# A hybrid transformer kernel: steps may cross iterations, 26 down products formed from parts, low parts shared out anew

## Chip, cores and metric

One core of a Trainium2 chip runs the whole kernel in one launch. The metric is the device time of one execution in microseconds (us). The engines are TensorE (PE, with its weight loads listed as PEld), VectorE (DVE), ScalarE (ACT), GpSimd (POOL) and SyncE (SP, which only issues DMAs here).

## What is computed

The input is x of 8 sequences by 512 tokens by 128 channels, in float32. The reference, cut to its frame:

```
x = x + attention(layernorm(x))       # one causal head, d = 128
x = x + ffn(layernorm(x))             # layer 0
x = x + rwkv_block(layernorm(x))      # time mixing (wkv recurrence), then channel mixing, residual inside
x = x + ffn(layernorm(x))             # layer 1, the same weights as layer 0

ffn(x): softmax router over 32 experts, the top 4 with a capacity limit; each expert is
        (silu(x W1) * (x W3)) W2 * weight, with W1, W3 of 128x64 and W2 of 64x128;
        plus a shared expert of hidden width 128
```

## The kernel before

**Units and iterations.** Two experts are put side by side to make a hidden width of 128, so a feed-forward layer is 16 pairs plus the shared expert: 17 *units* (`UNITS`). One *iteration* `g` of 0 to 15 is the feed-forward layer of one sequence: g = 0 to 7 is layer 0 of the eight sequences, 8 to 15 is layer 1. All pairs are computed for all 512 tokens, with the routing weight multiplied in (it is zero where an expert was not chosen).

**One unit** goes through the engines so: TensorE forms the gate product in bank `pa` and the linear product in bank `pb` (`up`, L1039, L1040, L1043); ScalarE applies SiLU to `pa` (L732; or tanh, L734, after which VectorE completes it, L1449); VectorE multiplies by `pb` (`gate`, L1468 or L1471, giving `m_v`); GpSimd multiplies by the routing weights (`unit`, L587, giving `m_h`). The down product with W2 is then added up in the one bank `py` over the 17 units (`out_product`, L1045).

**Float32 by parts.** A product is either *plain* (a float32 matmul, which the trace lists as two matmul instructions, `py<-m_h,...` L1067) or *from parts*: each operand is a high part in `fp32r` plus a low remainder, and three `fp32r` matmuls are added, high by high, low weight by high, high weight by low (L1072, L1073, L1074). All up products are from parts. For a down product from parts the hidden tile has to be divided first: ScalarE copies `m_h` to the high part `m_hh` (`split_high`, L909, instruction at L921) and VectorE or GpSimd subtracts it to get the low part `m_hl` (`split_low`, L412, instruction at L416). A plain down product needs neither. `NATIVE[g]` lists the units with plain down products: 88 of the 272 before. `LOW_ON_POOL[g]` lists the units whose low part is GpSimd's, if they have one (64 of the 184 divided units; 120 are VectorE's). `LOW_LATE[g]` says which of VectorE's low parts stand after the unit's gate instead of before it, and `TANH[g]` which units use tanh (52).

**Rings.** `m_h` has 5 buffers, `m_hh` and `m_hl` have 3 each; the high part is made two units behind (`SPLIT_LAG`), the down product stands four units behind (`LAG`). Up products of unit p wait for the SiLU and the gate of unit p-2.

**Everything else is interleaved by hand.** Beside the units, an iteration carries other sequences' steps, as `plan(g)` says: attention of sequence g+2 (g < 6), the routing of iteration g+1 (`pro`), the begin, finish and out of time mixing (`begin`, `finish`, `out`), channel mixing (`cmix`). Each engine's program is written in *slots*: three to a unit (`PARTS`), 54 to an iteration (51 on TensorE). Every step has a tuple with one slot number for each of its occurrences, and is issued in that engine's queue when the loop comes to that slot. Before, the steps of `plan(g)` could only stand in iteration g. An engine runs its queue in order, so a step that waits for a semaphore holds what is behind it. Ahead of the iterations stands the *opening*, 40 slots of its own: the attention of sequences 0 and 1, the routing of sequence 0, the division of the weights into parts (`weights_step`) and the first two units' up products (`first_step`). `keep_clock` puts filler matmuls in the opening (22 in all by `FILL`); the fillers are not changed.

**DMA.** All loads and stores are issued on SP's queue in a fixed order that has no slots: input 0, w1, w3, input 1, the gate matrix, w2 and so on; then for every iteration the routing weights go out and come back broadcast over partitions.

**Functions that the change's steps touch:** `iteration` on each of four engines (L677, L936, L1346, L1805), `att_step` (L1482 on VectorE), `weights_step` (L1509 on VectorE, L611 on GpSimd), `pro_step`, `time_begin`, `time_finish`, `time_out`, `channel_step`, `first_step`.

## Time and profile before

| what | value |
|---|---|
| median of 3 runs | 792.92 us (792.66 to 793.96) |
| span of the profiled execution | 791.7 us (no other time is given for it) |
| PE busy | 785.1 us, 99% of the span |
| DVE, POOL, ACT busy | 645.9 (82%), 625.3 (79%), 567.9 us (72%) |
| mean granted TensorE clock | 1.000 of full speed |
| moved by DMA | 80.73 MB, mean 102 GB/s |

A busy share is the time in which an engine has an instruction under way, also where that instruction waits for a resource after it has begun. Matmuls are pipelined: the time given for one matmul holds the passage through the array, so the distance from the start of one to the start of the next, where neither waits, tells what it costs. Where an instruction follows a long one, its listed start can lie before the moment at which its columns enter, and the start after it has to be used.

### The profile page before, as it was taken

The numbers are of one execution on the slowest core, as the hardware profiler recorded it, in microseconds if no ns is written. First come the engines' busy times: TensorE is split into PE (matmuls) and PEld (weight loads), VectorE is DVE, ScalarE is ACT, GpSimd is POOL, SyncE is SP. The second block draws the span as 40 slices with busy tenths as digits, with TensorE's granted clock in tenths as the row PEclk, the third lists the DMA queues.
The fourth block names the chain that finished last, engine by engine and source line by source line (L and its number), as shares of the span: only waits on it lengthen the run. The fifth ranks groups of instructions, "written<-read, shape, count | busy, mean of one in ns | idle before, by whom it ended". The sixth has DMA issues, their size and how long they took to land.

```text
span 791.7 us, 12780 instructions
## 1 busy us (share of the span) xinstructions
PE 785.1 (99%) x3817; PEld 596.4 (75%) x3817; DVE 645.9 (82%) x1539; ACT 567.9 (72%) x1055; POOL 625.3 (79%) x491
## 2 busy tenths in 40 slices
PE   8999999999999999999999999999999999999998
PEld 5777778676776777768778777887778767788786
DVE  6875577997997989998988869988689889767686
ACT  5677787868768778689765867668685775677553
POOL 6687779849767797769987888998797877876985
PEclk9999999999999999999999999999999999999999
DMA  9353334243144342462425444253444424425552
GB/s 326 95 123 82 87 92 113 66 102 92 42 113 113 73 105 54 110 133 58 120 60 134 104 93 107 65 143 79 110 113 95 90 68 110 111 59 115 124 127 74
DMA packets 49332, 80.73 MB, mean 102 GB/s; under 512 B 3280, under 2 KB 14544, under 8 KB 48880
## 3 DMA queue, kind: packets, MB, share of 16 engines
q1 hardware_dynamic: 48976, 79.72, 42.1%
q8 instruction: 31, 0.51, 0.3%
q14 instruction: 37, 0.30, 0.1%
q10 hardware_dynamic: 288, 0.20, 0.1%
HBM read 75.19 MB, written 4.72 MB: 101 GB/s over the span
## 4 chain that ended last, share of the span: by engine, by line
PE 51%; POOL 2%; issue 2%; DVE 1%; ACT 0%; DVEq 0%; POOLq 0%; ACTq 0%
PE pa L1039 5%; PE pb L1039 4%; PE py L1067 4%; PE pa L1043 4%; PE pb L1043 4%; PE pa L1040 4%; PE pb L1040 4%; PE pu L1326 4%; PE py L1072 3%; PE py L1074 3%; PE py L1073 3%; POOL m_h L587 1%; PE pq L1283 1%; PE pu L1310 1%; PE pv L1334 1%
## 5 line engine op out<-in xcount | busy, mean ns | idle before, releaser
L587 POOL TENSOR_TENSOR m_h<-m_v,m_wb 128x512 f32<-128x512 f32 x254 | 364.3, 1444 | 98.7 <-DVE m_v L1468 42.9
L732 ACT ACTIVATE m_th<-pa 128x512 f32<-128x512 f32 x220 | 130.6, 594 | 102.0 <-PE pa L1043 97.7
L1468 DVE TENSOR_TENSOR m_v<-m_th,pb 128x512 f32<-128x512 f32 x205 | 138.6, 679 | 23.9 <-ACT m_th L732 15.5
L1039 PE MATMUL pa<-m_xh,w1h 128*128 128x512 f32 x272 | 137.2, 504 | 0.3 <-DVE m_v L1471 0.2
L416 DVE TENSOR_TENSOR m_hl<-m_h,m_hh 128x512 fp32r<-128x512 f32 x120 | 111.4, 929 | 24.8 <-ACT m_hh L921 24.1
L921 ACT ACTIVATE m_hh<-m_h 128x512 fp32r<-128x512 f32 x184 | 115.2, 626 | 13.8 <-POOL m_h L587 13.1
L1039 PE MATMUL pb<-m_xh,w3h 128*128 128x512 f32 x272 | 115.4, 424 | 0.0
L1043 PE MATMUL pa<-m_xl,w1h 128*128 128x512 f32 x272 | 107.3, 394 | 0.3 <-POOL m_xl L608 0.3
L1043 PE MATMUL pb<-m_xl,w3h 128*128 128x512 f32 x272 | 107.1, 394 | 0.0
L1040 PE MATMUL pa<-m_xh,w1l 128*128 128x512 f32 x272 | 106.6, 392 | 0.0
L1040 PE MATMUL pb<-m_xh,w3l 128*128 128x512 f32 x272 | 106.5, 391 | 0.0
L416 POOL TENSOR_TENSOR m_hl<-m_h,m_hh 128x512 fp32r<-128x512 f32 x64 | 86.1, 1345 | 12.6 <-ACT m_hh L921 12.1
L1072 PE MATMUL py<-m_hh,w2h 128*128 128x512 f32 x183 | 77.2, 422 | 0.0
L1074 PE MATMUL py<-m_hl,w2h 128*128 128x512 f32 x183 | 72.0, 394 | 0.0
L1073 PE MATMUL py<-m_hh,w2l 128*128 128x512 f32 x183 | 71.6, 392 | 0.0
L1039 PEld LDWEIGHTS pa<-m_xh,w1h 128*128 128x128 f32 x272 | 51.5, 189 | 25.5 <-issue 14.4
L1040 PEld LDWEIGHTS pa<-m_xh,w1l 128*128 128x128 f32 x272 | 51.5, 189 | 20.6 <-issue 14.6
L1039 PEld LDWEIGHTS pb<-m_xh,w3h 128*128 128x128 f32 x272 | 51.3, 189 | 14.0 <-issue 3.9
L1043 PEld LDWEIGHTS pa<-m_xl,w1h 128*128 128x128 f32 x272 | 51.1, 188 | 12.2 <-POOL m_xl L608 0.7
L1043 PEld LDWEIGHTS pb<-m_xl,w3h 128*128 128x128 f32 x272 | 51.1, 188 | 11.6
L1040 PEld LDWEIGHTS pb<-m_xh,w3l 128*128 128x128 f32 x272 | 51.4, 189 | 10.8 <-issue 1.9
L1449 DVE SCALAR_TENSOR_TENSOR m_th<-m_th,pa 128x512 f32<-128x512 f32 x52 | 35.2, 677 | 15.9 <-ACT m_th L734 15.8
(318 smaller groups left out, 1653.8 us busy)
## 6 DMA issues: line engine op xcount, KB each, us to landing
m_wb<-w_scratch SPq DMA_DIRECT2D x126, 512.0 KB, 6.5
x_sb<-in_x SPq DMA_DIRECT2D x8, 256.0 KB, 7.2
m_wb<-in_w SPq DMA_DIRECT2D x2, 1024.0 KB, 6.8
x_out<-x_sb SPq DMA_DIRECT2D x7, 256.0 KB, 6.6
u_scratch<-t_u SPq DMA_DIRECT2D x6, 256.0 KB, 2.6
t_u<-u_scratch SPq DMA_DIRECT2D x6, 256.0 KB, 2.7
f_kk<-in_w SPq DMA_DIRECT2D x1, 1024.0 KB, 9.7
w_scratch<-r_wT SPq DMA_DIRECT2D x16, 64.0 KB, 1.5
```

The lines of the kernel that those rows point to most:

```text
L416: eng.tensor_tensor(m_hl[:, at, :], hidden(g, p), m_hh[:, at, :].bitcast(F32), ALU.subtract)\
L587: pool.tensor_tensor(hidden(g, p), gated(g, p), m_wb[:, p % (GRING * GP), :], ALU.mult).then_inc(sig["m_h"], 1)
L732: ins = act.activation(m_th[:, p % 2, :], pa[p % 2][:, :], ACT.Silu)
L921: act.activation(m_hh[:, halves_at(g, p), :], hidden(g, p), ACT.Copy).then_inc(sig["m_hh"], 1)
L1039: pe.matmul(ps[:, :], high[:, p, :], xh, start=True, stop=False)
L1040: pe.matmul(ps[:, :], low[:, p, :], xh, start=False, stop=False)
L1043: return pe.matmul(ps[:, :], high[:, p, :], xl, start=False, stop=True)
L1072: pe.matmul(py[:, :], w2h[:, p, :], hh, start=(p == 0), stop=False)
L1073: pe.matmul(py[:, :], w2l[:, p, :], hh, start=False, stop=False)
L1074: pe.matmul(py[:, :], w2h[:, p, :], hl, start=False, stop=(p == last_down(g))).then_inc(sig["m_y"], 1)
L1449: dve.scalar_tensor_tensor(out=m_th[:, r, :], in0=m_th[:, r, :], scalar=1.0, in1=pa[r][:, :], op0=ALU.add, op1=ALU.mult).then_inc(sig["m_u ...
L1468: dve.tensor_tensor(gated(g, p), m_th[:, r, :], pb[r][:, :], ALU.mult).then_inc(sig["m_v"], 1)
```

## The change

New is `STAGE`, the 54 slots of an iteration. Each engine's `iteration` no longer runs the steps of its own plan alone but also those of the plans before and after, with the slot moved by 54: a slot below 0 stands in the iteration ahead, one of 54 or more in the iteration behind.

```diff
+STAGE = PARTS * (UNITS + 1)
...
+def beside(g):
+
+    return tuple((plan(g + d), -d * STAGE) for d in (-1, 0, 1) if 0 <= g + d < 2 * B)
...
-                    if it.att is not None:
-                        att_step(it.att, slot)
...
+                    for near, shift in beside(g):
+                        if near.att is not None:
+                            att_step(near.att, slot + shift)
```

Nearly every slot tuple is new. On VectorE, where most crossings are:

```diff
             def att_step(n, slot):
-                if slot == (0, 7, 8, 1, 1, 11, 9, 13)[n]:
+                if slot == (2, 6, 6, -42, -34, 9, 8, -18)[n]:
                     if n < 2:
                         dve.wait_ge(sig["in_x1" if n else "in_x0"], 16)
                     row_stats(chunk(n), a_st, a_mv, n, "a_stats", "a_mvs")
...
-                if slot == (2, 10, 14, 8, 16, 16, 21, 19)[n]:
+                if slot == (6, 9, 11, -9, 11, 15, 16, 19)[n]:
                     dve.wait_ge(sig["a_rstd"], n + 1)
                     if n == 0:
                         normalise(a_xn, chunk(n), a_mv, a_rq, "a_xn")
...
-                if slot == (3, 21, 23, 28, 34, 28, 33, 33)[n]:
+                if slot == (7, 22, 27, 24, 32, 30, 34, 31)[n]:
                     row_max(n, 0, (0, 1), (0, P))
...
-                if slot == (16, 48, 51, 50, 52, 53, 49, 51)[n]:
+                if slot == (14, 43, 49, 49, 58, 60, 63, 57)[n]:
                     add_att(n, 2, (3,))
...
             def weights_step(slot):
 
-                if slot == (2,)[0]:
+                if slot == (3,)[0]:
                     high_part(w1h[:, 0:PAIRS, :], w_stage[:, 0:PAIRS, :], "in_w1")
-                if slot == (12,)[0]:
+                if slot == (10,)[0]:
                     high_part(w3h[:, 0:PAIRS, :], w_stage[:, PAIRS:2 * PAIRS, :], "in_w3")
-                if slot == (20,)[0]:
+                if slot == (10,)[0]:
                     high_part(w2h[:, 0:PAIRS, :], w2_stage, "in_w2")
...
-                if slot == (16,)[0] and q == 0:
+                if slot == (12,)[0] and q == 0:
 
                     dve.wait_ge(sig["a_add"], 2)
                     for t in range(T - 1):
                         dve.bn_stats(r_st[:, t, :], chunk(0)[:, t, :])
...
-                if slot == (52, 49, 52, 52, 45, 47, 50, 53)[m]:
+                if slot == (55, 56, 59, 53, 46, 48, 49, 59)[m]:
                     dve.wait_ge(sig["t_ri"], T * m + T)
                     dve.wait_ge(sig["t_num"], m + 1)
                     dve.tensor_tensor(t_ri[:, :], t_n1[:, :], t_ri[:, :], ALU.mult).then_inc(sig["t_y"], 1)
```

The lists of plain down products and of low parts (some iterations of `NATIVE`; `LOW_ON_POOL` and `LOW_LATE` change likewise):

```diff
 NATIVE = (
-    (3, 9),
-    (11,),
-    (2, 3, 5, 6, 9, 10, 11, 12, 13),
-    (1, 2, 3, 4, 5, 7, 9, 10, 11, 12, 13, 14, 15),
...
+    (3, 12),
+    (),
+    (2, 3, 9, 10, 11, 12, 13, 14),
+    (1, 2, 3, 4, 5, 7, 9, 10, 13, 14, 15),
...
```

Counted over all iterations, after against before:

| | before | after |
|---|---|---|
| plain down products | 88 | 62 |
| divided units (down products from parts) | 184 | 210 |
| low parts on DVE | 120 | 141 |
| low parts on POOL | 64 | 69 |
| units with tanh | 52 | 52 |

Plain products by iteration g = 0 to 15: before 2, 1, 9, 13, 9, 8, 6, 5, 7, 5, 6, 5, 6, 2, 2, 2; after 2, 0, 8, 11, 6, 7, 3, 3, 6, 3, 4, 4, 3, 0, 1, 1. VectorE's low parts by iteration: before 7, 9, 7, 3, 5, 6, 9, 7, 7, 5, 7, 9, 7, 9, 11, 12; after 9, 11, 9, 3, 7, 6, 10, 7, 8, 7, 8, 10, 9, 10, 13, 14.

## Rows read from the trace of the kernel before

**Rows 1.** The profile page: busy time, share of the span and instructions of each engine.

```profile
PE 785.1 (99%) x3817; PEld 596.4 (75%) x3817; DVE 645.9 (82%) x1539; ACT 567.9 (72%) x1055; POOL 625.3 (79%) x491
```

**Rows 2.** Waits of TensorE and its weight loads: us in total, times, longest.

```profile
PE pa L1039 <- DVE m_v L1471: 0.2, 1, 0.2
...
PEld pa L1039 <- DVE m_v L1471: 2.8, 7, 1.1
...
PEld py L1072 <- ACT m_hh L921: 0.9, 2, 0.7
```

**Rows 3.** Chain that ended last, in its final microseconds: start, us, what.

```profile
784.02 0.23 PE py L1072
...
784.71 1.72 PE py L1067 x4
```

**Rows 4.** Timeline of TensorE: start us, us, line, operation, tiles, shapes, count.

```profile
403.52 0.39 PE L1040 MATMUL pa<-m_xh,w1l 128*128 128x512 f32 x1
...
404.66 1.02 PE L1067 MATMUL py<-m_h,w2f 128*128 128x512 f32 x2
...
405.75 0.39 PE L1040 MATMUL pa<-m_xh,w1l 128*128 128x512 f32 x1
```

**Rows 5.** Instructions of three lines: duration ns min/median/max, first and last start us.

```profile
L416 DVE TENSOR_TENSOR m_hl<-m_h,m_hh x120: 671/693/1792, 41.0 to 786.3; 128x512 fp32r<-128x512 f32 x120
L416 POOL TENSOR_TENSOR m_hl<-m_h,m_hh x64: 1262/1294/1760, 37.6 to 781.8; 128x512 fp32r<-128x512 f32 x64
...
L587 POOL TENSOR_TENSOR m_h<-m_v,m_wb x254: 1260/1300/2208, 38.9 to 784.4; 128x512 f32<-128x512 f32 x127
...
L921 ACT ACTIVATE m_hh<-m_h x184: 612/624/672, 36.9 to 785.7; 128x512 fp32r<-128x512 f32 x184
```

**Rows 6.** Windows of three iterations: us; busy of PE, PEld, DVE, ACT, POOL; clock; DMA; GB/s.

```profile
222.00:273.00 51.00, 51.00 (x242) 37.08 (x241) 44.53 (x113) 39.40 (x73) 37.23 (x28) 1.00 0.31 79
273.00:324.00 51.00, 51.00 (x243) 37.51 (x243) 46.21 (x110) 39.10 (x73) 41.65 (x32) 1.00 0.45 102
612.00:665.00 53.00, 52.75 (x255) 39.71 (x254) 47.13 (x102) 37.00 (x69) 43.29 (x33) 1.00 0.32 77
```

**Rows 7.** Timeline of VectorE, then of GpSimd, near the end.

```profile
776.73 1.48 DVE L416 TENSOR_TENSOR m_hl<-m_h,m_hh 128x512 fp32r<-128x512 f32 x1
778.36 1.55 DVE L416 TENSOR_TENSOR m_hl<-m_h,m_hh 128x512 fp32r<-128x512 f32 x1 [0.15 <-ACT m_hh L921]
...
777.61 1.76 POOL L587 TENSOR_TENSOR m_h<-m_v,m_wb 128x512 f32<-128x512 f32 x1
```

**Rows 8.** Two loads of the opening, with their time from issue to landing.

```profile
L476 SPq DMA_DIRECT2D m_wb<-in_w x1: 509/509/509, 1.3 to 1.3; - x1
...
DMA to landing us min/median/max: 5.8/5.8/5.8
...
L478 SPq DMA_DIRECT2D x_sb<-in_x x1: 433/433/433, 2.3 to 2.3; - x1
...
DMA to landing us min/median/max: 8.2/8.2/8.2
```

**Rows 9.** Timeline of VectorE in the opening.

```profile
7.26 1.12 DVE L1440 TENSOR_SCALAR a_xn<-x_sb,a_q,a_rq 128x128 f32<-128x128 f32 x4 [1.14 <-POOL a_rq L572]
8.29 1.22 DVE L1531 CAST w1h<-m_wb 128x2048 fp32r<-128x2048 f32 x1
10.57 0.62 DVE L1541 TENSOR_REDUCE a_nm<-pv 128x1 f32<-128x128 f32 x2 [1.06 <-PE pv L1158]
...
13.15 0.86 DVE L1416 BATCH_NORM_STATS2 a_st<-x_sb 128x6 f32<-128x128 f32 x4
...
14.65 0.15 DVE L1556 RECIPROCAL a_ri<-a_sum 128x2 f32<-128x2 f32 x1
...
18.07 0.35 DVE L1560 SCALAR_TENSOR_TENSOR x_sb<-pb,a_ri,x_sb 128x128 f32<-128x128 f32 x1
18.34 0.67 DVE L1570 BATCH_NORM_STATS2 r_st<-x_sb 128x6 f32<-128x128 f32 x3
```

More of the change, by code:

```diff
@@ L124 @@
     (),
-    (1, 2, 3, 4, 7, 9, 12),
+    (1, 2, 4, 7, 9, 12),
 )
@@ L686, in iteration @@
                             split_low(pool, *before, "m_hl_pool")
[L687 to L694 removed]
+                    for near, shift in beside(g):
+                        if near.att is not None:
+                            att_step(near.att, slot + shift)
+                        if near.cmix is not None:
+                            channel_step(near.cmix, slot + shift)
+                        if near.begin is not None:
+                            time_begin(near.begin, slot + shift)
+                        if near.pro is not None:
+                            pro_step(near.pro, slot + shift)
             for slot in range(OPENING):
@@ L947, in iteration @@
                         att_step(1, OPENING + slot)
-                    if it.att is not None:
-                        att_step(it.att, slot)
-                    if it.cmix is not None:
-                        channel_step(it.cmix, slot)
-                    if it.pro is not None:
-                        pro_step(it.pro, slot, it.cmix)
-                    if it.begin is not None:
-                        time_begin(it.begin, slot, it.pro)
+                    for near, shift in beside(g):
+                        if near.att is not None:
+                            att_step(near.att, slot + shift)
+                        if near.cmix is not None:
+                            channel_step(near.cmix, slot + shift)
+                        if near.pro is not None:
+                            pro_step(near.pro, slot + shift, near.cmix)
+                        if near.begin is not None:
+                            time_begin(near.begin, slot + shift, near.pro)
             for slot in range(OPENING):
@@ L1249, in spread_step @@
             def spread_step(slot):
-                if slot == (34,)[0]:
+                if slot == (37,)[0]:
                     pe.wait_ge(sig["r_wT"], 1)
@@ L1359, in iteration @@
                         att_step(1, OPENING + slot, None, False)
-                    if it.att is not None:
-                        att_step(it.att, slot, g, it.begin is not None)
-                    if it.out is not None:
-                        time_out(it.out, slot, it.pro)
-                    if it.cmix is not None:
-                        channel_step(it.cmix, slot, it.pro)
-                    if it.pro is not None:
-                        pro_step(it.pro, slot, it.begin, it.cmix)
-                    if it.begin is not None:
-                        time_begin(it.begin, slot, it.pro, it.cmix)
+                    for near, shift in beside(g):
+                        if near.att is not None:
+                            att_step(near.att, slot + shift, near.g, near.begin is not None)
+                        if near.out is not None:
+                            time_out(near.out, slot + shift, near.pro)
+                        if near.cmix is not None:
+                            channel_step(near.cmix, slot + shift, near.pro)
+                        if near.pro is not None:
+                            pro_step(near.pro, slot + shift, near.begin, near.cmix)
+                        if near.begin is not None:
+                            time_begin(near.begin, slot + shift, near.pro, near.cmix)
             for slot in range(OPENING):
@@ L1823, in iteration @@
                         att_step(1, OPENING + slot)
-                    if it.att is not None:
-                        att_step(it.att, slot)
-                    if it.out is not None:
-                        time_out(it.out, slot)
-                    if it.begin is not None:
-                        time_begin(it.begin, slot)
-                    if it.finish is not None:
-                        time_finish(it.finish, slot)
-                    if it.pro is not None:
-                        pro_step(it.pro, slot, it.cmix)
-                    if it.cmix is not None:
-                        channel_step(it.cmix, slot)
+                    for near, shift in beside(g):
+                        if near.att is not None:
+                            att_step(near.att, slot + shift)
+                        if near.out is not None:
+                            time_out(near.out, slot + shift)
+                        if near.begin is not None:
+                            time_begin(near.begin, slot + shift)
+                        if near.finish is not None:
+                            time_finish(near.finish, slot + shift)
+                        if near.pro is not None:
+                            pro_step(near.pro, slot + shift, near.cmix)
+                        if near.cmix is not None:
+                            channel_step(near.cmix, slot + shift)
             for slot in range(OPENING):
```

370 lines of the change are left out of this document (188 added, 182 removed), and 12 rows, old and new, of the table NATIVE.

## Prediction, made before the changed kernel ran

> **What bounds the kernel now.** I read the page's busy line first: TensorE is busy 785.1 of 791.7 us and the next engine, VectorE, 82% [rows 1]. "Busy" alone doesn't prove a bound, so the waits come next. TensorE itself waits for another engine about once in the steady part, 0.2 us [rows 2]. Its weight loads, which run ahead of the matmuls, wait a little more: 2.8 us in all for VectorE's gate and 0.9 us in all for ScalarE's high part, the longest of these 0.7 us [rows 2]. So outside the opening the matmuls stand end to end, and what is saved on TensorE shortens the kernel unless another engine then comes late.
>
> What one matmul costs has to be read from distances. In the chain that ended last a matmul of a product from parts stands for 0.23 us, and four instructions of two plain products for 1.72 us, so 0.86 us for a plain product [rows 3]. The timeline agrees in mid-kernel: from one `pa` L1040 at 403.52 us to the next at 405.75 us there are 2.23 us, and they hold six matmuls from parts and one plain product [rows 4]. With 0.86 for the plain one, 1.37 us is left for six, 0.228 each. The durations listed there (0.39 and 1.02 us) contain the passage through the array and aren't the cost.
>
> **The change, part by part.**
>
> *Down products.* 26 plain products go (88 to 62) and 26 times three matmuls come. Removed: 26 x 0.86 = 22.4 us. Added: 26 x 3 x 0.228 = 17.8 us. Net -4.5 us, wholly on TensorE, so on the path. One of the 26 is unit 13 of the last iteration, in the tail; its hidden tile is made well before its product, so I count it like the others.
>
> *What the 26 need.* 26 high parts on ScalarE at 0.62 us = 16.2 us. 21 more low parts on VectorE at the median of 0.69 us = 14.6 us, and at 1.55 us, which one took when GpSimd stood against it, 32.6 us. 5 more on GpSimd at 1.29 us = 6.5 us [rows 5, 7]. None of this is on the path while it is ready when its product comes. ScalarE goes from 72 to 74%, GpSimd from 79 to 80%, VectorE from 82 to 84% (86% at the bound) of the span. The cover is the lag of four units between up and down product; a unit is 51 to 53 us / 17, near 3 us [rows 6], so 12 us. After the gate the hidden tile needs 1.30 us on GpSimd, 0.62 on ScalarE and 0.7 to 1.3 us for the low part [rows 5], 2.6 to 3.2 us. If SiLU and gate take as much again, over 5 us are left for queueing. If the cover went, each late low part would stall TensorE directly, since the product stands in TensorE's queue ahead of the next unit's up products.
>
> *Low parts shared out anew.* The tightest stretches of VectorE are iterations 4, 5 and 12, busy 44.5 and 46.2 of 51 us and 47.1 of 53 us [rows 6] (the third busy column there). Iterations 4 and 12 get 2 more low parts each (+1.4 us), iteration 5 none.
>
> *Steps across iterations.* They cost nothing by themselves: no instruction is added. On VectorE, iteration 12 gives the statistics of time mixing's start to iteration 11 and its last two multiplications (slots 59 and 64) to iteration 13. Iteration 4 gives up several microseconds of time mixing's finish (slots 56 to 62), but mostly to iteration 5, which is the fuller one. So iteration 12 is relieved and the pair 4 and 5 is not: together 90.7 of 102 us before, 92.1 after, or 90%. DMA issues have no slots, and their queue keeps its order; stores and reloads move only with the semaphores that they wait for.
>
> For the stalls of the steady part I have no row, so bounds. Below: the gains end when all the waits of rows 2 are gone, -3.9 us. Above: 13 of the 26 new low parts are in iterations 2 to 6 and 12; if every one came one port wait late (next paragraph, 0.8 us), +10.4 us. I take +0.5 us, near the small waits that are there now, since the margin of 5 us is larger than any single wait seen.
>
> *The shared port.* Near the end a VectorE low part took 1.48 us, a GpSimd multiplication begun during it 1.76 us, and the VectorE low part begun during that one 1.55 us, against medians of 0.69 and 1.30 us [rows 5, 7]. They end one after the other: at 778.21, 779.37 and 779.91 us. So each added low part is paid for twice, on its own engine and as a delay of up to about 0.8 us on the other. The Trainium skill ("SBUF — State Buffer", Who interferes with whom) says why: a VectorE instruction with two SBUF inputs and a GpSimd instruction that reads SBUF take a shared read interface, and the later one blocks fully. By that rule the change is worse than its busy shares say, because it adds 21 instructions of just that form; the trace agrees, with the numbers above. The sum by busy shares alone would have no stall term; by the rule at its worst it is the slower rival below.
>
> *The opening.* VectorE now makes w1's high part (slot 3) ahead of the normalisation of sequence 0 (slot 6). w1 is issued at 1.3 us and lands 5.8 us later, at 7.1 us [rows 8]. The normalisation began at 7.26 us and the cast takes 1.22 us [rows 9], so the normalisation begins at 8.3 us, 1.0 us late. Then the statistics of sequence 1 (slot 6) stand ahead of the first row maximum (slot 7). They wait for input 1, issued at 2.3 us and landing 8.2 us later, at 10.5 us [rows 8]. Statistics and moments fill 13.15 to 14.65 us now, 1.5 us [rows 9], so the row maximum moves from 10.57 to 12.0 us: +1.5 us on the chain of sequence 0's attention. Given back: three of four tiles' statistics for the router (0.67 us after the third add, 18.34 us [rows 9]) now stand ahead of that add, at slot 12, while TensorE still forms its values; and w3's cast no longer stands between the first and the third add, worth an estimated 0.4 us. +1.5 - 0.7 - 0.4 = +0.4 us. Ends: -1.0 us, if the new order takes out more idle time later than it costs, and +1.5 us, if nothing is given back.
>
> *Sum* against the profiled execution: 791.7 - 4.5 + 0.5 + 0.4 = 788.1 us of span. The median of the runs is 792.92 us, 1.2 us above that span, and I carry the distance over: **789.3 us**.
>
> **Rivals.**
>
> *The freedom pays beyond the products.* Crossing steps fill VectorE's and GpSimd's holes so well that the waits of rows 2 go and the opening gains 1 us. For it: the opening's VectorE queue has gaps of about 1 us, as the 1.06 us ahead of the first row maximum [rows 9]. Against: TensorE has little left to gain. 791.7 - 4.5 - 3.9 - 1.0 + 1.2 = 783.5 us in full; about half of these gains, 786, is more likely.
>
> *The gain is swallowed: no change.* The opening costs its full 1.5 us and small waits of TensorE take 2 us more in the denser iterations 4 to 6 (six to eight products late by 0.3 us). 792.9 - 4.5 + 1.5 + 2 = 791.9 us. For it: the landing time of input 1, which no reordering can change.
>
> *Slower: the port becomes the bound.* Place: the down product's wait for `m_hl`, in iterations 2 to 6 and 12; in 4, 5 and 12 VectorE is 87 to 91% busy now [rows 6]. One port wait of 0.8 us on each of the 13 new low parts, unhidden, is +10.4 us: 792.9 - 4.5 + 0.4 + 10.4 = 799.2 us. It decides from 0.32 us a product on (4.1 us over 13). For it: the staggered ends of rows 7. Against: the lag leaves 5 us, and before the change TensorE waits for VectorE or ScalarE almost nowhere although GpSimd and VectorE already collide.
>
> That the change doesn't do what it says I don't count: the lists give the 26 products.
>
> **How the numbers follow.** My forecast has 0.55 (788 to 791.2 us), the larger gain 0.14, no change 0.15, slower 0.16. About 0.2%, 1.6 us, is what a measurement of this kernel can tell from no change. Faster takes the forecast and the larger gain: 0.69. The range runs from 786 us, the halved larger gain, to 794.5 us, where the slower case has begun (under half of its waits, 4.6 us, and the full opening); about 0.06 lies below and 0.11 above.
>
> **What would show it.** Right: 62 plain and 210 divided down products; TensorE's sum of costs down by 4.5 us; plain and part matmuls still 0.86 and 0.23 us apart; median times of `m_hl` as before. Opening: the first row maximum near 12 us instead of 10.57, the first up product later than now, but behind more attention work. Wrong: waits of TensorE or its weight loads for `m_hl`, `m_hh` or `m_v` that sum to over 4 us, or a first row maximum before 11 us.

## The result: 850.4 us instead of 793.0, slower by 7%

| | before | after |
|---|---|---|
| median of 4 runs on the same chip | 793.01 us | 850.4 us (849.75 to 851.3) |
| ratio | | 1.0719 [1.0704, 1.0734] |
| span of the profiled execution | 791.7 us | 848.9 us |

The forecast was 789.3 us, with 794.5 us as the upper end of its range. The truth lies 56 us outside of it. The busy line of the page after, beside [rows 1]:

```profile
PE 804.6 (95%) x3843; PEld 598.7 (71%) x3843; DVE 703.1 (83%) x1560; ACT 584.8 (69%) x1083; POOL 651.7 (77%) x496
```

The instruction counts are those of the plan. But VectorE is busy 57.2 us longer for 21 more low parts, which I had priced at 14.6 us, and TensorE is now only 95% busy. The busy time of TensorE tells little here (a matmul that runs at a lower clock is busy longer). So I counted as in the prediction: each matmul at its distance to the next (0.2285 us for one of three parts, 0.43 for each instruction of a plain product, the others likewise), and what stands between matmuls beyond that as a gap. The demand fell from 778.8 to 775.1 us, which is the -4.5 us of the forecast within this count's accuracy. The gaps rose from 7.8 to 58.0 us. So the expected gain is there, and 50 us of new waiting lie over it. The rest of the difference, some 10 us, I put down to matmuls at the lower clock: the mean granted clock fell from 1.000 to 0.990, which over 848.9 us is worth about 8 us.

What TensorE and its weight loads wait for after, beside [rows 2] (us in total, times, longest):

```profile
PE pv L1342 <- DVE r_lg L1602: 5.2, 2, 3.7
PE pa L1047 <- DVE m_v L1480: 5.2, 7, 1.8
PE pb L1047 <- DVE m_v L1477: 5.1, 11, 0.9
PE pu L1181 <- ACT a_p L791: 4.8, 5, 2.0
PE pu L1318 <- DVE a_pT L1789: 2.8, 2, 1.8
...
PE py L1080 <- POOL m_hl L422: 1.7, 3, 0.8
...
PEld pb L1047 <- DVE m_v L1477: 17.7, 34, 1.4
...
PEld pa L1047 <- DVE m_v L1480: 10.7, 15, 2.2
...
PEld pu L1181 <- ACT a_p L791: 9.3, 10, 2.4
```

The weight loads' waits for the gate `m_v` went from 2.8 us [rows 2] to over 28 us. The waits are short and many, and most lead to VectorE: to its gate, its router steps, its blends. The softmax step `a_p` is ScalarE's, but ScalarE in turn waits 11.1 us for VectorE's row maximum `a_nm` there (4.3 before). The down product with its low part, the place on which both my forecast and my slower rival had their eye, accounts for 1.7 us. The loss is also spread: the 16 iterations took between 3 us less and 8 us more than before.

Why VectorE is late shows in single instructions. The low part and two steps of channel and time mixing, by line, after and then before (busy us, mean ns; idle us ahead of them):

```profile
L422 DVE TENSOR_TENSOR m_hl<-m_h,m_hh 128x512 fp32r<-128x512 f32 x141 | 135.3, 959 | 23.9 <-ACT m_hh L928 22.9
L1789 DVE SCALAR_TENSOR_TENSOR a_pT<-a_g,vec,a_xT 128x512 f32<-128x512 f32 x8 | 14.2, 1769 | 0.0
L1709 DVE TENSOR_TENSOR_SCAN t_bb<-t_ea 128x512 f32<-128x512 f32 x8 | 13.2, 1651 | 0.0
```

```profile
L416 DVE TENSOR_TENSOR m_hl<-m_h,m_hh 128x512 fp32r<-128x512 f32 x120 | 111.4, 929 | 24.8 <-ACT m_hh L921 24.1
L1780 DVE SCALAR_TENSOR_TENSOR a_pT<-a_g,vec,a_xT 128x512 f32<-128x512 f32 x8 | 7.3, 912 | 0.0
L1700 DVE TENSOR_TENSOR_SCAN t_bb<-t_ea 128x512 f32<-128x512 f32 x8 | 9.8, 1221 | 0.0
```

The eight blends `a_pT` are the same eight instructions in both kernels. Before, nearly all ran unhindered (median 746 ns, longest 1774); after, all eight took 1748 to 1785 ns. One place of the timeline after shows the cause, VectorE first and then GpSimd:

```profile
740.86 1.57 DVE L1789 SCALAR_TENSOR_TENSOR a_p<-a_g,vec,a_xT 128x512 f32<-128x512 f32 x1
742.35 1.78 DVE L1789 SCALAR_TENSOR_TENSOR a_pT<-a_g,vec,a_xT 128x512 f32<-128x512 f32 x1
744.06 1.77 DVE L1756 TENSOR_TENSOR f_xl<-a_p,f_xh 128x512 fp32r<-128x512 f32 x1
...
740.60 1.28 POOL L593 TENSOR_TENSOR m_h<-m_v,m_wb 128x512 f32<-128x512 f32 x1
741.83 1.75 POOL L422 TENSOR_TENSOR m_hl<-m_h,m_hh 128x512 fp32r<-128x512 f32 x1
743.55 1.73 POOL L593 TENSOR_TENSOR m_h<-m_v,m_wb 128x512 f32<-128x512 f32 x1
745.24 1.74 POOL L614 TENSOR_TENSOR m_xl<-t_v,m_xh 128x512 fp32r<-128x512 f32 x1
```

Read the ends: 741.88 (GpSimd), 742.43, 743.58 (GpSimd), 744.13, 745.28 (GpSimd), 745.83. The two engines take turns. Each instruction runs for about 0.55 us (VectorE) or 1.15 us (GpSimd) after the other's end, and both engines look 100% busy, though alone such instructions take about 0.75 and 1.28 us. It is the collision of [rows 7], now as a steady state: while three such instructions follow one another, VectorE works at 1.7 us each instead of 0.7.

### The profile page after: what moved, and what is told of

The parts are those of the page before. It is cut to its first block and busy times, and to the rows that moved or that the text cites. A ratio compares the mean times of both kernels' runs of the same rounds, so it can differ in the third digit from the quotient of the medians.

```text
span 848.9 us, 12914 instructions
## 1 busy us (share of the span) xinstructions
PE 804.6 (95%) x3843; PEld 598.7 (71%) x3843; DVE 703.1 (83%) x1560; ACT 584.8 (69%) x1083; POOL 651.7 (77%) x496
## 5 line engine op out<-in xcount | busy, mean ns | idle before, releaser
L593 POOL TENSOR_TENSOR m_h<-m_v,m_wb 128x512 f32<-128x512 f32 x254 | 375.4, 1486 | 115.7 <-DVE m_v L1477 46.9
L928 ACT ACTIVATE m_hh<-m_h 128x512 fp32r<-128x512 f32 x210 | 131.7, 627 | 39.6 <-POOL m_h L593 37.9
L422 DVE TENSOR_TENSOR m_hl<-m_h,m_hh 128x512 fp32r<-128x512 f32 x141 | 135.3, 959 | 23.9 <-ACT m_hh L928 22.9
L1047 PE MATMUL pa<-m_xh,w1h 128*128 128x512 f32 x272 | 135.0, 496 | 6.1 <-DVE m_v L1480 5.2
L1047 PE MATMUL pb<-m_xh,w3h 128*128 128x512 f32 x272 | 118.3, 435 | 6.8 <-DVE m_v L1477 5.1
L422 POOL TENSOR_TENSOR m_hl<-m_h,m_hh 128x512 fp32r<-128x512 f32 x69 | 96.6, 1400 | 16.0 <-ACT m_hh L928 16.0
L1080 PE MATMUL py<-m_hh,w2h 128*128 128x512 f32 x209 | 89.0, 426 | 2.5 <-POOL m_hl L422 1.7
L1082 PE MATMUL py<-m_hl,w2h 128*128 128x512 f32 x209 | 82.2, 393 | 0.0
L1081 PE MATMUL py<-m_hh,w2l 128*128 128x512 f32 x209 | 81.8, 391 | 0.0
L1047 PEld LDWEIGHTS pa<-m_xh,w1h 128*128 128x128 f32 x272 | 51.4, 189 | 32.9 <-issue 12.2
L1048 PEld LDWEIGHTS pa<-m_xh,w1l 128*128 128x128 f32 x272 | 51.4, 189 | 18.8 <-issue 12.7
L1051 PEld LDWEIGHTS pb<-m_xl,w3h 128*128 128x128 f32 x272 | 51.3, 189 | 12.0
L1080 PEld LDWEIGHTS py<-m_hh,w2h 128*128 128x128 f32 x209 | 39.3, 188 | 16.3 <-issue 6.9
```

Of the source, the lines that this page charges most:

```text
L422: eng.tensor_tensor(m_hl[:, at, :], hidden(g, p), m_hh[:, at, :].bitcast(F32), ALU.subtract)\
L593: pool.tensor_tensor(hidden(g, p), gated(g, p), m_wb[:, p % (GRING * GP), :], ALU.mult).then_inc(sig["m_h"], 1)
L928: act.activation(m_hh[:, halves_at(g, p), :], hidden(g, p), ACT.Copy).then_inc(sig["m_hh"], 1)
L1047: pe.matmul(ps[:, :], high[:, p, :], xh, start=True, stop=False)
L1048: pe.matmul(ps[:, :], low[:, p, :], xh, start=False, stop=False)
L1051: return pe.matmul(ps[:, :], high[:, p, :], xl, start=False, stop=True)
```

## The experiments

Unless said otherwise a kernel computes everything and differs from its neighbour only by the edit shown. "Before" ran beside them at 792.8 to 793.7 us. The kernels made from the one before carry the loop over three plans too, with its old slots, so that nothing moves by it (e6, with no instruction added, is within 2 us of before). Reasons open at the start: the lists (more low parts), the slots (other order), the opening; and beneath them the port, plain lack of slack, or waits in the product itself.

### Which part of the change costs

**Slots and lists, each alone.** `e1_old_lists` keeps the new slots and takes back the lists:

```diff
 NATIVE = (
-    (3, 12),
-    (),
+    (3, 9),
+    (11,),
...
```

> The changed kernel with the four lists of before (88 plain down products, 120 and 64 low parts); all slots are new. Theory P (the new slot numbers cost the time; the 26 products gain): VectorE and GpSimd have 26 low parts fewer, TensorE 4.5 us more to do; 845 to 856 us. Theory L (the 21 + 5 added low parts overload VectorE and the port it shares with GpSimd, the slots cost little but the opening's 8.7 us): near 800 us.

Measured: 844.08 us, 1.0653 [1.0614, 1.0692]. `e2_old_slots` is the reverse, all slot tuples of before with the new lists:

```diff
-                if slot == (2, 6, 6, -42, -34, 9, 8, -18)[n]:
+                if slot == (0, 7, 8, 1, 1, 11, 9, 13)[n]:
...
```

> The kernel before with the four lists of the change: 26 down products from parts, all slots as before. Theory P: 788 to 793 us, for the products save 4.5 us and the denser queues give at most some of it back. Theory L: 830 to 842 us, as the changed kernel without its slow opening. VectorE's busy time: P says 645.9 + 15 to 20 us, L says about 700 us.

Measured: 822.92 us, 1.0383 [1.0365, 1.04]. So the new order alone costs 51.3 us with not one instruction added (the opening's share, below, is part of it), and the lists alone 30.1 us, where I had forecast a gain. Together they cost 57, not 81: the two overlap. The busy lines of e1 and of e2:

```profile
PE 809.1 (95%) x3817; PEld 596.2 (70%) x3817; DVE 684.0 (81%) x1539; ACT 572.4 (68%) x1057; POOL 630.9 (74%) x491
```

```profile
PE 791.5 (97%) x3843; PEld 599.3 (73%) x3843; DVE 676.4 (83%) x1560; ACT 580.2 (71%) x1081; POOL 640.1 (78%) x496
```

In e1 VectorE has the 1539 instructions of before and is busy 38.1 us longer [rows 1]. The order alone made its instructions longer; the blend `a_pT` of above takes 14.2 us here too.

**The opening.** `e3_old_opening` is the changed kernel with the opening's slots of before on every engine, `e4_new_opening` the kernel before with those of after (e4's edit of VectorE's statistics and cast; e3's is the reverse):

```diff
-                if slot == (0, 7, 8, 1, 1, 11, 9, 13)[n]:
+                if slot == (2, 6, 8, 1, 1, 11, 9, 13)[n]:
...
-                if slot == (2,)[0]:
+                if slot == (3,)[0]:
                     high_part(w1h[:, 0:PAIRS, :], w_stage[:, 0:PAIRS, :], "in_w1")
...
```

> The changed kernel with the opening's slots of before (attention of sequences 0 and 1, routing of sequence 0, the weights' parts, first units). If the opening costs what the first up product's start says (32.9 against 24.2 us) and nothing later absorbs it: 850.4 - 8.7 = 841.7 us (840 to 843.5), with the first up product at 24 us. If the delay is taken up later (the chain that ended last doesn't pass through the opening): 848 to 851 us.

> The kernel before with the opening's slots of the change, nothing else. If the opening's loss is of the opening alone: 793.0 + 8.7 = 801.7 us (800 to 803.5). By my blind estimate of +0.4 us it would be 793.4. The four normalisations of sequence 0 should take 4.0 us instead of 1.12 us, beside GpSimd's low parts of w1.

Measured: e3 846.04 us, 1.0675 [1.0659, 1.069], 4.4 us better than after; e4 799.64 us, 1.0083 [1.0068, 1.0098], 6.9 us worse than before. Forecast from the first up product's start were 8.7 us in both; the steady part takes up some of the delay, in the changed kernel about half. The opening is a real cost of its own, and about a tenth of the whole. Where it starts shows VectorE's timeline in e4, beside [rows 9]:

```profile
7.30 1.23 DVE L1540 CAST w1h<-m_wb 128x2048 fp32r<-128x2048 f32 x1 [0.96 <-DMA m_wb<-in_w]
8.45 4.04 DVE L1449 TENSOR_SCALAR a_xn<-x_sb,a_q,a_rq 128x128 f32<-128x128 f32 x4
12.41 0.86 DVE L1425 BATCH_NORM_STATS2 a_st<-x_sb 128x6 f32<-128x128 f32 x4
...
15.71 0.62 DVE L1550 TENSOR_REDUCE a_nm<-pv 128x1 f32<-128x128 f32 x2 [1.72 <-PE pv L1166]
```

The cast ahead of the normalisations releases GpSimd's low quarters of w1 (before, they began at 9.59 us, behind the normalisations), and the four normalisations, a tile each, then take 4.04 us instead of 1.12 [rows 9]. In the changed kernel the same pair stands so:

```profile
8.82 4.04 DVE L1449 TENSOR_SCALAR a_xn<-x_sb,a_q,a_rq 128x128 f32<-128x128 f32 x4
```

```profile
8.98 3.79 POOL L649 TENSOR_TENSOR w1l<-m_wb,w1h 128x512 fp32r<-128x512 f32 x3 [1.90 <-DVE w1h L1540]
```

Meanwhile TensorE (the changed kernel again, here and in the window below) turns one tile each 1.2 us, and its following matmuls are slow as well:

```profile
11.67 0.33 PE L995 MATMUL pu<-ident,a_xn 128*128 128x128 f32 x1 [0.92 <-DVE a_xn L1449]
12.91 0.48 PE L995 MATMUL pu<-ident,a_xn 128*128 128x128 f32 x1 [0.91 <-DVE a_xn L1449]
...
15.83 1.59 PE L1165 MATMUL pa<-a_xT,a_g 128*128 128x384 f32 x2
```

The pair of 384 columns that took 0.86 us before takes 1.59 us. The window of these microseconds shows why, in its column for the granted clock (the third from the end), which was 1.00 in the same stage before:

```profile
14.00:20.00 6.00, 5.93 (x17) 3.21 (x18) 2.68 (x11) 2.91 (x11) 2.25 (x2) 0.58 1.10 335
```

For most of that stretch the clock stood at 1.2 instead of 2.4 GHz, after the waits of 0.9 us between single matmuls. The first up product comes at 32.9 us instead of 24.2 (32.6 in e4).

To test the collision, `e12_opening_low_later` is e4 with GpSimd's four quarters of w1 all at slot 14 (they were at 7, 8, 11 and 13), nothing else moved:

```diff
-                if slot == (7,)[0]:
+                if slot == (14,)[0]:
                     low_quarter(1, w1l, w1, w1h, 1)
...
```

> e4_new_opening (799.6 us) with GpSimd's four low quarters of w1 not before slot 14, behind its reciprocal root of sequence 1; the other engines' order is the same. If GpSimd's low parts blocked the four normalisations of sequence 0 on the shared port (4.0 instead of 1.1 us): the normalisations take 1.1 us again and 2.5 to 3.5 us come back, 796 to 797.5 us. If their time was the wait for w1's load: 799 to 801 us.

Measured: 799.15 us, 1.0073 [1.0056, 1.009], the time of e4. Yet VectorE's part did what the collision predicts:

```profile
8.48 1.11 DVE L1449 TENSOR_SCALAR a_xn<-x_sb,a_q,a_rq 128x128 f32<-128x128 f32 x4
...
12.31 0.61 DVE L1550 TENSOR_REDUCE a_nm<-pv 128x1 f32<-128x128 f32 x2
```

The first row maximum comes at 12.31 us, where I had forecast 12.0. So the collision is shown as the cause of the 4.04 us, but not as the cause of the opening's loss: the time is what the other theory had named. GpSimd now makes quarters of w1 and w3 from 13.46 to 24.5 us, and behind them in its queue stands the root `r_q` for the routing, whose input is ready at 21.05 us. GpSimd first, then VectorE:

```profile
24.48 1.03 POOL L578 TENSOR_TENSOR r_q<-r_ve,minus_half 128x4 f32<-128x4 f32 x1
```

```profile
25.55 1.11 DVE L1449 TENSOR_SCALAR t_k<-x_sb,r_q 128x128 f32<-128x128 f32 x4 [4.49 <-POOL r_q L578]
```

VectorE waits 4.49 us for it, and the first up product comes at 32.9 us as before the edit. In the kernel before, GpSimd had made the four quarters of w1 between 9.59 and 14.6 us, while VectorE took its row maxima from TensorE's banks. The earlier cast and the later quarters both give up that place. What a good place for them would be in the new order wasn't tried.

### Lists: the products or the low parts?

`e5_native_only` (old slots, only `NATIVE` new) and `e6_share_only` (old slots and `NATIVE`; new `LOW_ON_POOL`, `LOW_LATE`, `TANH`) split the lists. First e5's, then e6's edit of the kernel before:

```diff
 NATIVE = (
-    (3, 9),
-    (11,),
+    (3, 12),
+    (),
...
```

```diff
 LOW_ON_POOL = (
-    (0, 2, 3, 7, 8, 9, 11, 12, 13, 14),
-    (3, 4, 7, 10, 11, 13, 14, 15),
+    (0, 2, 3, 7, 9, 11, 12, 14),
+    (3, 7, 10, 13, 14, 15),
...
```

> Slots and the other three lists as before; only the list of plain down products is the change's (62 instead of 88), so the new divided units take the engine that the old lists name. Theory N (it is the 26 extra high and low parts that make VectorE and GpSimd late, by more than their own duration because they collide on the shared port): 815 to 830 us, as e2_old_slots (822.9). Theory S (it is the sharing out anew of the low parts that were there before, against slots that were fitted to the old sharing): 788 to 796 us.

> Slots and plain down products as before; only LOW_ON_POOL, LOW_LATE and TANH are the change's, so no instruction is added but some low parts change engine or place in VectorE's queue. Theory N: 790 to 800 us. Theory S: 812 to 825 us. If both contribute alike, each near 805 us.

Measured: e5 821.46 us, 1.0354 [1.0339, 1.037]; e6 795.2 us, 1.0024 [1.0014, 1.0034]. This sharing out among the engines costs little (+2.0 us); dividing 28 units more (2 others became plain, net 26) costs 28.3 us.

`e11_divided_plain` keeps all of e5's high and low parts but gives the 28 units their plain product, so that TensorE waits for no part of them (VectorE and GpSimd still do, before they write to that unit's buffer again, five units on); `e13_high_only` takes out their low parts too and keeps the high ones:

```diff
-                if native(g, p):
+                if native(g, p) or p in STILL_PLAIN[g]:
...
```

```diff
-                if g >= 0 and not native(g, p) and not low_on_pool(g, p):
+                if g >= 0 and not native(g, p) and not low_on_pool(g, p) and p not in STILL_PLAIN[g]:
...
```

> e5_native_only (821.5 us), where the high and low parts of the 28 newly divided units are still made, at the same places, but TensorE forms their down products plainly and doesn't wait for them (two units are plain in both). TensorE has 28 x 0.17 = 4.8 us more to do. If the time is lost because the product waits for a late low part: 795 to 805 us. If it is lost because the instructions themselves hold up the queues of ScalarE, VectorE and GpSimd: 822 to 828 us.

> e11_divided_plain (819.9 us) without the low parts of the 28 newly divided units: ScalarE still copies their high parts (28 x 0.63 us, each waiting for GpSimd's product), VectorE and GpSimd do what they did before, TensorE forms these products plainly. If VectorE's and GpSimd's added low parts are what costs: 793 to 799 us. If ScalarE's high parts hold up its queue: 808 to 820 us.

Measured: e11 819.9 us, 1.0336 [1.032, 1.0351]; e13 796.57 us, 1.0042 [1.0027, 1.0057]. This is the cleanest cut of the study, because no matmul of e11 reads the 28 low parts and still they cost 819.9 - 796.6 = 23.3 us, 0.83 us each. The 28 high parts cost 3.4 us. TensorE has 28 x 0.17 = 4.8 us less to do in e5 than in e11, and yet e5 is 1.6 us slower; so waits of the products for late parts cost about 6.4 us, an estimate from two runs on different chips. Most of the low parts' cost is thus not that they come late for their own product: they hold back what comes after them. The lines of the low parts, high parts and `m_h` in e11 and e13:

```profile
L595 POOL TENSOR_TENSOR m_h<-m_v,m_wb 128x512 f32<-128x512 f32 x254 | 366.6, 1451 | 104.8 <-DVE m_v L1479 46.4
L424 DVE TENSOR_TENSOR m_hl<-m_h,m_hh 128x512 fp32r<-128x512 f32 x136 | 131.6, 969 | 36.0 <-ACT m_hh L930 35.4
```

```profile
L598 POOL TENSOR_TENSOR m_h<-m_v,m_wb 128x512 f32<-128x512 f32 x254 | 364.4, 1444 | 102.5 <-DVE m_v L1483 44.5
L427 DVE TENSOR_TENSOR m_hl<-m_h,m_hh 128x512 fp32r<-128x512 f32 x120 | 110.3, 920 | 26.0 <-ACT m_hh L934 25.0
```

16 more low parts on VectorE are 21.3 us more of busy time, 1.33 us each, and 10 us more of standing idle ahead of one for its high part. That idle time is VectorE's own queue held up: what stands behind the low part, the next gate among it, can't start.

**Does the price depend on how full the iteration is?** `e14_light` divides only the 11 new units of iterations 0, 1, 5, 8 to 11, 14 and 15, `e15_heavy` only the 17 of iterations 2, 3, 4, 6, 7, 12 and 13 (both as e5, with `NATIVE` of before in the other iterations). Iterations 2 and 3 in e14:

```diff
-    (2, 3, 9, 10, 11, 12, 13, 14),
-    (1, 2, 3, 4, 5, 7, 9, 10, 13, 14, 15),
+    (2, 3, 5, 6, 9, 10, 11, 12, 13),
+    (1, 2, 3, 4, 5, 7, 9, 10, 11, 12, 13, 14, 15),
...
```

> The kernel before, where only the 11 newly divided units of iterations 0, 1, 5, 8, 9, 10, 11, 14 and 15 are formed from parts (e5_native_only had 28 and lost 28.3 us). If each costs the same 1.0 us: 804 us. If the price depends on how full VectorE and GpSimd already are: 791 to 798 us, and what these 11 save on TensorE (1.9 us) may show.

> The kernel before, where only the 17 newly divided units of iterations 2, 3, 4, 6, 7, 12 and 13 are formed from parts. At an equal price: 810 us. If the price depends on the load: 815 to 822 us. With e14_light the losses should add up to that of e5_native_only (28 us) if they don't influence each other.

Measured: e14 801.58 us, 1.0106 [1.0091, 1.0121], +8.4 us or 0.76 each; e15 812.88 us, 1.0245 [1.0228, 1.0263], +19.7 us or 1.16 each. The sum, 28.1 us, is e5's 28.3. Both lie between the two forecasts. Fuller iterations charge more, but even the light ones, taken together, have no room to give: the gain of 0.17 us a product doesn't show in them. Single iterations weren't tried.

### How much of it is the port?

The four "lone" kernels replace VectorE's low part by an instruction with one SBUF input:

```diff
+            if signal == "m_hl_dve":
+                eng.tensor_scalar(m_hl[:, at, :], hidden(g, p), 0.0, None, ALU.mult, ALU.add,
+                                  accum_out=low_sum[:, at:at + 1]).then_inc(sig[signal], 1)
+                return
```

In them VectorE's low parts are zero, so that share of the down products is missing; waits, slots and all other instructions stay. e7 edits e2, e8 edits the changed kernel, e10 edits e1, and e9 the kernel before, as the control.

> e2_old_slots (822.9 us) with VectorE's 141 low parts written by an instruction that reads only one SBUF tensor (the hidden tile times 0, with its sum taken along) instead of two: same place, same waits, about the same duration alone. It leaves out the low part of the hidden tile, which becomes zero. Theory P (collision on the port shared with GpSimd): the low part takes 0.7 us always, GpSimd's mean falls too, and TensorE's gaps shrink: 795 to 808 us. Theory Q (the queues are simply too full or in the wrong order; the port is a side show): 817 to 825 us.

> The changed kernel (850.4 us) with the same edit: VectorE's 141 low parts read one SBUF tensor and become zero. Theory P: VectorE's busy time falls from 703 by 40 us or more, 815 to 832 us. Theory Q: VectorE's busy time falls somewhat, the time stays at 843 to 852 us, since other late steps take over.

> Control for the one-input edit: the kernel before with VectorE's 120 low parts written from one SBUF input (they become zero, the low part of the hidden tile is left out). TensorE has few waits there to give up, so if the edit has no effect of its own: 789 to 793 us. If it fell by 10 us or more, the falls seen in e7_lone_old_slots (-14.4) and e8_lone_after (-27.2) would not be about the added collisions.

> New slots, old lists (844.1 us) with the one-input edit. In that run VectorE's busy time was 38 us above before with the same instructions. If collisions on the shared port are what the new slots cost: 812 to 825 us, VectorE's busy time down to 650. If the order of the steps costs by waits alone: 838 to 846 us.

| VectorE's low part | two SBUF inputs | one SBUF input | difference |
|---|---|---|---|
| before | 793.5 | e9 792.13, 0.9986 [0.9977, 0.9996] | -1.4 |
| new lists, old slots (e2) | 822.92 | e7 808.49, 1.0193 [1.0178, 1.0208] | -14.4 |
| old lists, new slots (e1) | 844.08 | e10 822.43, 1.0368 [1.0349, 1.0387] | -21.7 |
| after | 850.4 | e8 823.2, 1.0373 [1.0355, 1.039] | -27.2 |

The new instruction takes 679 ns, nearly alike every time (665 to 689 in e8), instead of 929 to 981 on average, though a read of its accumulator of 0.08 us comes with each, and GpSimd's `m_h` is shorter too, here in e7:

```profile
L424 DVE TENSOR_SCALAR_CACHE_REDUCE m_hl<-m_h 128x512 fp32r<-128x512 f32 x141 | 95.6, 679 | 33.2 <-ACT m_hh L933 32.5
...
L598 POOL TENSOR_TENSOR m_h<-m_v,m_wb 128x512 f32<-128x512 f32 x254 | 345.8, 1369 | 112.9 <-DVE m_v L1482 41.9
```

Four readings. First, the port is real, and taking VectorE's low parts off it gives back about half of each loss. Second, the control: in the kernel before the same edit takes 31.7 us of busy time off VectorE and 25.9 off GpSimd (page of e9 against [rows 1]: 614.2 and 599.4 us), and the time moves by 1.4 us. Before, what these low parts' collisions cost was all but hidden. Third, about 15 us stay in e7, 29 in e10 and 30 in e8. In e10 and e8 it contains the opening, which the edit doesn't touch and which alone cost 4.4 to 6.9 us. Fourth, this rest isn't free of the port either: only VectorE's low parts were changed, and in e10 the blend is as slow as ever:

```profile
L1794 DVE SCALAR_TENSOR_TENSOR a_pT<-a_g,vec,a_xT 128x512 f32<-128x512 f32 x8 | 14.2, 1779 | 0.0
```

What part of the rest is the port and what is order isn't told apart by these runs.

One more candidate for the rest stands in the waits, and no run tests it. GpSimd waits for the routing weights `m_wb` to come back from memory at the start of an iteration. Before, then after (us in total, times, longest):

```profile
POOL m_h L587 <- DMA m_wb<-w_scratch: 12.3, 5, 3.1
```

```profile
POOL m_h L593 <- DMA m_wb<-w_scratch: 35.1, 11, 6.0
```

It is 37.1 us in e1, 39.6 in e10, 34.8 in e17 and 20.5 in e18, but 17 to 22 in e2, e5 and e7, so it goes with the new slots and the one-input edit doesn't lower it. VectorE's gate in turn waits until GpSimd has taken the tile of two units before (4.4 us in all before, 8.2 after, 7.0 in e10). Against it stands the place of the longest such wait in e10, 6.5 us up to 238.5 us: TensorE waits for nothing between 228 and 262 us there.

### A stall in full

The longest gap of e2 shows how port and queue order combine. ScalarE, GpSimd, VectorE and TensorE from 328 to 336 us:

```profile
328.55 1.28 ACT L739 ACT_TABLE_LOAD   x1
329.85 0.60 ACT L739 ACTIVATE m_th<-pa 128x512 f32<-128x512 f32 x1
330.34 0.62 ACT L928 ACTIVATE m_hh<-m_h 128x512 fp32r<-128x512 f32 x1
```

```profile
331.04 1.50 POOL L422 TENSOR_TENSOR m_hl<-m_h,m_hh 128x512 fp32r<-128x512 f32 x1 [1.31 <-ACT m_hh L928]
332.50 1.27 POOL L670 TENSOR_TENSOR t_xv<-t_eb,t_v 128x512 f32<-128x512 f32 x1
```

```profile
333.81 1.74 DVE L1725 TENSOR_TENSOR t_n<-t_n,t_xv 128x512 f32<-128x512 f32 x1 [1.81 <-POOL t_xv L670]
335.47 0.67 DVE L1477 TENSOR_TENSOR m_h<-m_th,pb 128x512 f32<-128x512 f32 x1
```

```profile
336.20 0.67 PE L1047 MATMUL pb<-m_xh,w3h 128*128 128x512 f32 x1 [2.35 <-DVE m_h L1477]
```

A low part on GpSimd waits 1.31 us for ScalarE's high part, which stood behind a table load there. It holds up `t_xv`, a step of time mixing. VectorE stands 1.81 us before `t_n`, which reads `t_xv`, and then takes 1.74 us for it, against GpSimd. The gate stands behind that in VectorE's queue, and TensorE waits 2.35 us for the gate. No step of this chain concerns the late low part's own product. The matmul at 336.20 also shows 0.67 us where its like takes 0.48 (the one at 332.90): after the wait the granted clock is 0.55 on average from 336 to 339.5 us.

### Are the slots' 51 us in one place?

`e16_root_later` moves one step of the changed kernel, GpSimd's root for the last routing, which had been put ahead by an iteration and held its queue for 4.8 us in e1:

```diff
-                if slot == (17, 11, 3, 5, 8, 7, 8, 10, 5, 7, 4, -1, 3, 1, 8, -5)[q]:
+                if slot == (17, 11, 3, 5, 8, 7, 8, 10, 5, 7, 4, -1, 3, 1, 8, 2)[q]:
```

> The changed kernel (850.4 us) with one slot altered: GpSimd's reciprocal root for the routing of iteration 15 goes from slot -5 (in iteration 13's end, 5 slots ahead of VectorE's moments that it waits for) to 2. In e1_old_lists GpSimd stood 4.8 us at this step. If a step ahead of its producer costs what its engine waits there: 845 to 847.5 us. If the time is lost anyway, because the same dependency is waited for further on or other waits take over: 849 to 851.5 us.

Measured: 849.56 us, 1.0701 [1.0685, 1.0717], 0.8 us better. GpSimd's waits at these roots went from 5.6 to 3.2 us in all, and almost nothing came of it.

`e17_first_half` is the kernel before with the new slots for the steps of iterations 0 to 7, `e18_second_half` with those for 8 to 15 (lists and opening of before). One line of e17, on VectorE, and one of e18, on GpSimd:

```diff
-                if slot == (0, 7, 8, 1, 1, 11, 9, 13)[n]:
+                if slot == (0, 7, 6, -42, -34, 9, 8, -18)[n]:
...
-                if slot == (20, 10, 6, 7, 4, 4, 7, 11, 5, 1, 7, 7, 9, 4, 6, 0)[q]:
+                if slot == (20, 10, 6, 7, 4, 4, 7, 11, 5, 7, 4, -1, 3, 1, 8, -5)[q]:
...
```

> The kernel before (lists and opening too) with the new slots for the steps of iterations 0 to 7 only. New slots with old lists lost 51.3 us, of it 4 to 7 in the opening, so 45 are left. Spread evenly: half of it, 812 to 820 us. By the iteration lengths of e1_old_lists: iterations 1 to 7 were 27 us longer than before, and 0 in its own slots. A few misplaced steps of the second half alone: under 800 us.

> The kernel before with the new slots for the steps of iterations 8 to 15 only. Spread evenly: 812 to 820 us; if the halves don't influence each other, the losses of this run and of e17_first_half add up to about 45 us.

Measured: e17 814.08 us, 1.0249 [1.0231, 1.0266], +20.4 us; e18 820.04 us, 1.0322 [1.0296, 1.0348], +26.3 us. With the opening's 6.9 us that is 53.6, beside e1's 51.3. So the loss is not in one place: the opening and each half of the new table bring their part of it. VectorE's busy time rises in each (662.1 and 658.6 us, from 645.9), by 16.2 and 12.7 us.

Not tried: the 92 slot entries that cross an iteration apart from the other 1061 that changed, or one engine's slots alone. The tables of the four engines are matched to each other, and a mixture can wait in a circle. So it stays open whether crossing as such costs anything, or only this table.

## Why the prediction was wrong, step by step

1. **Down products, -4.5 us: right.** TensorE's demand fell by 3.7 us in my count, and plain and part matmuls cost what they did.

2. **"None of this is on the path while it is ready when its product comes": this failed, for +28 to +30 us.** I measured the cover by the wrong distance. The 12 us lag between up and down product protects the product that reads the low part, and e11 shows that this was nearly right: waits for late parts cost 6.4 us in all. But an added instruction also pushes back everything behind it on its engine. Behind VectorE's low part stands the next gate, and TensorE may run only two units ahead of the gate. That is the lag which had to be weighed; that it is this one which decides is read from the waits for `m_v` and the program, for no run changed it. [rows 2] already named the place: the weight loads waited 2.8 us for `m_v` and 0.9 us for `m_hh`. I read the small sum as slack. It can as well be read as a sign that the loads were already touching VectorE. The prices: a low part 0.83 us, a high part 0.12 us, against a gain of 0.17 us for a product. My +0.5 us of stalls stands against some 28 us, and the bound of +10.4 us, though built from the right collision, counted 13 products and not all 28, and one delay at the wrong place.

3. **VectorE at 82 to 84% of the span, read as room: this failed with step 2.** The idle time was not room: in the kernel before VectorE stood idle for 24.1 us ahead of its 120 low parts, waiting for ScalarE's high parts, and what stands behind them in its queue can't fill that. The margin of 5 us a unit was an average, and the waits come from the moments at which two engines and a queue order meet.

4. **"They cost nothing by themselves: no instruction is added": failed, for 44 to 47 us in the steady part (e1 less the opening; e17 and e18 together).** This was the largest error. An order decides how often VectorE's instructions meet GpSimd's at the port. With all instructions the same, VectorE's busy time grew by 38 us (e1), and taking its low parts off the port gave 21.7 us back (e10). Why the rest is lost stays open. I had the collision in the rows, with its price, and used it for the added low parts only. Comparing busy shares of iterations 4, 5 and 12 couldn't show it, and after the change those iterations are not special: VectorE is busy 52.0, 50.5 and 47.6 us in stretches of 54, 54 and 59 us,

```profile
235.00:289.00 54.00, 52.38 (x251) 37.68 (x250) 51.95 (x113) 38.12 (x74) 42.60 (x30) 1.00 0.39 92
289.00:343.00 54.00, 51.06 (x236) 35.89 (x234) 50.46 (x114) 39.26 (x74) 42.60 (x33) 1.00 0.34 77
655.00:714.00 59.00, 55.28 (x260) 42.23 (x259) 47.55 (x95) 40.77 (x74) 44.95 (x34) 0.94 0.34 75
```

   where [rows 6] had 44.5, 46.2 and 47.1. In iteration 4 that is 7.4 us more for two more low parts.

5. **Opening, +0.4 us: failed, 4.4 to 6.9 us.** The late cast and the statistics ahead of the row maximum were sized right (12.0 forecast, 12.31 in e12, where nothing collides with the normalisations). What I left out is GpSimd: the earlier cast releases its quarters of w1 right beside the normalisations, which then take 4.04 us instead of 1.12, and put later (e12) the quarters hold up the root for the routing by 3.4 us. The Trainium skill ("SBUF — State Buffer", Who interferes with whom) says that not only two inputs lead to the shared port: copies, casts and TENSOR_SCALAR can run in a mode that takes it too, but not the form of TENSOR_SCALAR that also writes out its accumulator. The trace agrees: the four normalisations, with one SBUF tensor as input, were slowed as said, and the accumulator form was not (665 to 689 ns in e8). I had taken the rule for two inputs alone.

6. **The slower rival** had the right mechanism and its sign, and got 0.16. Its place (the down product's wait for `m_hl`) was wrong, its size (+6 us net of 57) too. I argued against it with "before the change TensorE waits almost nowhere although GpSimd and VectorE already collide". The control e9 qualifies that sentence: before, the low parts' collisions were there and cost 1.4 us, so they fell where almost nothing waited for them. That they are harmless in one order says nothing of another order, and with nearly every slot new there was another. The moved steps should have had a bound from the port too. At 0.8 us a collision [rows 7] the 38 us of e1's busy time are 48 more of them among 1539 instructions (an estimate made with the result in hand), and nothing in my rows excluded so many.

None of the variants that compute everything beats the kernel before.

## What to carry to other kernels

An engine that waits for nobody is not proof that the others have slack: look at every lead in the loop, the shortest first (here two units to the gate), and not only at that of the added result. Before pricing an added instruction on a second engine at nothing, look for who stands behind it there, and don't take a small sum of waits (2.8 us here) for slack: the next low parts cost 0.83 us each. Where two engines share a port, their busy shares can't be added or compared with the span; a new order is a change of cost though no instruction is added, and has to be timed part by part, each new table alone, with the port edit on the old kernel beside it as a control.

## What the runs showed of the hardware that was not expected

- Two SBUF-reading engines in a steady exchange: with back-to-back work on both, VectorE's 0.67 us instruction and GpSimd's 1.27 us one each took 1.73 to 1.78 us, one end after the other.
- A float32 TENSOR_SCALAR of 128x128 with one SBUF tensor as input, four in 1.12 us alone, took four in 4.04 us beside GpSimd. The form that also writes an accumulator (TENSOR_SCALAR_CACHE_REDUCE, 128x512) took 665 to 689 ns in all of its 141 instructions of e8, in a kernel whose GpSimd was 75% busy.
- Even a four-column instruction can be held up: the eight TENSOR_SCALAR of `t_ve` (128x4), 0.16 us each at their shortest, went from 0.36 us on average before to 0.82 after, and up to 1.29 us. That GpSimd holds them up wasn't tested on their own.
- After waits of 0.9 us between single matmuls in the opening the granted clock was 0.58 from 14 to 20 us, and the pair of 384 columns and what follows it stood 1.39 us apart in e4 instead of 0.70 before. So a short run of small stalls cost more than their sum.
